# Window attention: scores and transposes in smaller array tiles, probabilities three quarters behind, work reordered

## The reference, cut to what matters

```python
x = roll(gn(x), (-3, -3))                       # cut in 7x7 windows: 16 * 64 of them
qkv = xw @ qkv_w.T + qkv_b                      # q, k, v: 12 heads of 16 channels
attn = einsum('bhnd,bhmd->bhnm', q * 16**-0.5, k) + bias[None] + mask
attn = softmax(attn, axis=-1)                   # 49 x 49 per head and window
out = einsum('bhnm,bhmd->bhnd', attn, v) @ proj_w.T + proj_b
x = x + roll(out, (3, 3))
```

## Time and profile before

| | us |
|---|---|
| median of 3 runs (4780.85 to 4781.38) | 4781.35 |
| profiled execution, its own time | 4778.66 |
| its span in the trace | 4776.7 |
| PE busy in the span | 4503.8 (94%) |
| DVE busy | 3946.8 (83%) |
| ACT busy | 2366.2 (50%) |
| POOL busy | 2379.3 (50%) |

### The profile page before, as it was taken

The page is one execution under the profiler, slowest core; times in us unless marked ns, Lnnn a source line. Parts: engine busy times, 40 slices in busy tenths (PEclk is TensorE's granted clock), DMA queues, the critical chain, the costliest instruction groups (busy, mean ns, idle before and its releaser), DMA issues. The chain is left out here.

```text
span 4776.7 us, 123308 instructions
## 1 busy us (share of the span) xinstructions
PE 4503.8 (94%) x42504; PEld 3833.8 (80%) x42504; DVE 3946.8 (83%) x7850; ACT 2366.2 (50%) x4594; POOL 2379.3 (50%) x2098
## 2 busy tenths in 40 slices
PE   0599999999999999999969999999999999999998
PEld 0488888888888888888857888888888888888887
DVE  6788888888888888888827888888888888888887
ACT  0244444444444444444415555555555656555565
POOL 1245554555555554555425555555555555555555
PEclk9999999999999999999969999999999999999999
DMA  8011111111111111111112222222222222222222
GB/s 341 21 38 39 39 41 38 38 39 39 41 37 39 39 41 37 39 40 41 34 40 67 69 68 69 69 67 71 67 70 69 68 68 69 70 68 70 67 70 59
DMA packets 397987, 285.95 MB, mean 60 GB/s; under 512 B 155355, under 2 KB 396235, under 8 KB 396747
## 3 DMA queue, kind: packets, MB, share of 16 engines
q1 hardware_dynamic: 395204, 283.19, 20.2%
q10 hardware_dynamic: 2736, 2.14, 0.1%
HBM read 120.34 MB, written 87.31 MB: 43 GB/s over the span
## 5 line engine op out<-in xcount | busy, mean ns | idle before, releaser
L882 POOL TENSOR_TENSOR E<-E,ri 128x588 f32<-128x588 f32 x512 | 646.3, 1262 | 1028.5 <-DVE ri L1107 1028.3
L602 PE MATMUL ps_o<-w,g_hi 128*128 128x384 f32 x2352 | 710.9, 365 | 5.9 <-DVE g_lo L542 4.1
L414 ACT ACTIVATE gF<-ps_g,b1f 128x512 f32<-128x512 f32 x588 | 404.7, 688 | 393.0 <-PE ps_g L633 390.7
L960 ACT ACTIVATE E<-L 128x588 f32<-128x588 f32 x512 | 356.1, 695 | 475.6 <-POOL L L888 242.5
L1097 DVE SCALAR_TENSOR_TENSOR L<-ps_s,bias 128x588 f32<-128x588 f32 x512 | 394.5, 770 | 178.0 <-PE ps_s L1241 161.9
L602 PE MATMUL ps_o<-w,g_lo 128*128 128x192 f32 x2352 | 534.8, 254 | 0.0
L1249 PE MATMUL ps_t<-ident,E 128*98 128x128 f32 x3072 | 441.3, 280 | 41.1 <-POOL E L882 41.1
L441 POOL TENSOR_TENSOR res<-xt,b2b 128x768 f32<-128x768 f32 x98 | 181.5, 1852 | 591.1 <-DVE x L490 591.1
L400 ACT ACTIVATE h_hi<-ps_h,hbias 128x512 fp32r<-128x512 f32 x196 | 123.1, 679 | 703.7 <-PE ps_h L617 703.7
L1249 PEld LDWEIGHTS ps_t<-ident,E 128*98 128x98 f32 x3072 | 313.4, 127 | 195.4 <-POOL E L882 108.3
L1241 PE MATMUL ps_s<-Kp,Q 64*64 64x196 f32 x6144 | 455.4, 342 | 2.7 <-DMA Kp<-K 2.7
(11 more groups left out here) (211 smaller groups left out, 12090.5 us busy)
## 6 DMA issues: line engine op xcount, KB each, us to landing
xs<-in_x SPq DMA_DIRECT2D x8, 4704.0 KB, 22.0
xt<-in_x SPq DMA_DIRECT2D x98, 384.0 KB, 3.4
x_cells<-x SPq DMA_DIRECT2D x784, 48.0 KB
xb<-x_cells SPq DMA_DIRECT2D x128, 294.0 KB
Vx<-V SPq DMA_DIRECT2D x512, 73.5 KB
out<-yo SPq DMA_DIRECT2D x128, 294.0 KB
Kp<-K SPq DMA_DIRECT2D x512, 49.0 KB, 1.9
Kp<-K SPq DMA_DIRECT2D x512, 24.5 KB, 1.8
```

Source lines behind the costliest of these rows:

```text
L414: act.activation(gF[f % 4][:, :], ps_g[:, f % 2, :], ACT.Gelu, bias=b1f[:, f:f + 1]).then_inc(s_gelu, 1)
L602: last = pe.matmul(dst, g[:, f, P * k:P * (k + 1)], w, start=(f == 0 and i == 0), stop=(f == FT - 1 and i == 1))
L882: pool.tensor_tensor(e, e, ri[p][:, :].unsqueeze(2).to_broadcast([P, HEADS, T]), ALU.mult)\
L960: act.activation(E[pp][:, :, :], L[pp][:, :, :], ACT.Exp).then_inc(s_ex, 1)
```

## The change

The scores are made in 32-row products of two heads (98 columns) instead of 64-row products of four (196): twelve products a quarter, in a first group of eight (head pairs at places 0, 3, 1, 4) and a second of four (places 2, 5), with the transposes between them. `PAIR_AT` says which head pair stands at which place. Two row groups that run together write to different banks of `ps_s`. The keys are spread over two heads' rows instead of four, so half as many DMAs with twice the rows each. The transposes take 64 rows (one window) each, window w to bank w of `ps_t`: twelve of 64 columns. The lag is three quarters. `mix` half 0 goes from p0 to p2, the second `turn` ahead of the values product of p0, the second `project` behind the values product of p1, the third and `values` half 0 behind that of p2. VectorE makes sums and reciprocals after the subtraction, the lower parts and the queries instead of before; GpSimd takes the maxima off before it multiplies; ScalarE copies PT before the exponentials. Banks and their waits follow. Weights, bias and the bias table are permuted on the way in. The core of the diff:

```diff
+PAIR_AT = (0, 4, 2, 1, 5, 3)
...
-            HB = HEADS // 3
-            QB = 256
+            HB = 2
+            SB = HEADS // 2 * T
...
-            OUT0, TURN, QK, VAL, OUT1 = 0, 1, 3, 6, 8
+            LAG = 3
+            TURN, KEYS, OUT0, QRY, VAL, OUT1 = 0, 2, 4, 5, 6, 8
...
+            def s_pair(j):
+                return ps_s[:, 2 * j // JP, T2 * (j % (JP // 2)):T2 * (j % (JP // 2) + 1)]
+            def pair_rows(g):
+                return slice(2 * HD * (g % PA), 2 * HD * (g % PA + 1)), g // PA
...
# GpSimd
+                        if is_unit(u):
+                            less_max(u, p)
                         if is_unit(pu):
                             norm(pu, pp)
-                        if is_unit(u):
-                            less_max(u, p)
...
# ScalarE, order in a quarter
+ evacuated 1 (p2); PT copy; E; upper 0, upper 1 (p0); evacuated 0 (p1); V copy (p3); oT; evacuated 2 (p2)
- E; evacuated 1 (p2); PT copy; evacuated 0 (p1); evacuated 2 (p2); V copy (p3); upper 0 (p0); oT; upper 1 (p0)
# VectorE, order in a quarter
+ L; mx; first heads less mx; lower 0, 1 (p0); queries_b (p1); sm, ri; finish 0, V copy (p2); finish 1 (p3)
- L; mx; sm, ri; first heads less mx; finish 0 (p0); lower 0, 1 (p0); queries_b (p1); V copy (p2); finish 1 (p3)
...
# TensorE
+                def scores(c, p, places):
+                    for j in places:
+                        rows, chunk = pair_rows(PAIR_AT[j])
+                        for w in range(2):
+                            last = pe.matmul(s_pair(j)[SLOT * w:SLOT * (w + 1)], Q[c][rows, chunk, 2 * p + w, :],
+                                             Kp[c][rows, chunk, :, 2 * p + w, :], start=True, stop=True)
+                    return last
...
                         if is_unit(lu):
                             pe.wait_ge(s_nm, k + 1)
                             upto(pe, s_ptc, k)
+                        if is_unit(u):
+                            if p == 0:
+                                pe.wait_ge(s_qkm, 3 * u + 3)
+                                pe.wait_ge(s_qb, u + 1)
+                                pe.wait_ge(s_kp[c], 16 * K_SPREADS * (i + 1))
+                            upto(pe, s_lg, UP * u + p)
+                            scores(c, p, (0, 3, 1, 4)).then_inc(s_scx, 1)
+                        if is_unit(lu):
                             for j in range(JP):
-                                last = pe.transpose(ps_t[0:T2, j // JB, P * (j % JB):P * (j % JB + 1)],
-                                                    E[lp][:, 2 * j:2 * j + 2, :].rearrange("p h m -> p (h m)"),
-                                                    ident[:, :])
+                                for w in range(2):
+                                    rows = slice(SLOT * w, SLOT * (w + 1))
+                                    last = pe.transpose(ps_t[0:T2, w, SLOT * j:SLOT * (j + 1)],
+                                                        E[lp][rows, 2 * j:2 * j + 2, :].rearrange("p h m -> p (h m)"),
+                                                        ident[rows, rows])
                             last.then_inc(s_pt, 1)
+                        if nxt and p == 0:
+                            pe.wait_ge(s_xb[1 - c], 16 * LOADS * (i + c + 1))
+                            for h in range(2):
+                                upto(pe, s_vc[h], v)
+                        if is_unit(u):
+                            pe.wait_ge(s_scx, UP * u + p + 1)
+                            scores(c, p, (2, 5)).then_inc(s_sc, 1)
-                        if is_unit(u - 1) and p == 0:
+                        if is_unit(u - 1) and p == 2:
                             mix(i, c, 0)
# then: turn 0, 1 (p0); project 0 (p1); values 1 (p3); values product; project 1 (p1); project 2, values 0 (p2); mix 1 (p3)
```

More of the change, by code:

```diff
@@ L935, in evacuated @@
                     v, d, m = 2 * i + c + 1, 1 - c, CHUNK_OF[step]
-                    full = ps_w(QK + step)[:, 0:UW].rearrange("p (w t) -> p w t", t=T)
+                    full = ps_qk(step)[:, 0:UW].rearrange("p (w t) -> p w t", t=T)
                     act.wait_ge(s_qk, 3 * v + step + 1)
@@ L991, in slot @@
                             last.then_inc(s_o, 1)
-                        if nxt and p == 0:
-                            upper(i, c, 1)
+                        if nxt and p == 2:
+                            evacuated(i, c, 2)
                 units(act, slot)
@@ L1166, in _ @@
                 pe.wait_ge(s_pad, 2)
-                def turn(i, c, h):
[L1171 to L1178, removed]
+                def scores(c, p, places):
[5 more added lines that the diff above has]
+                    return last
+                def turn(i, c, h):
+                    d, rows = 1 - c, CB if h else P
                     for p in range(UP):
@@ L1188, in project @@
                         pe.wait_ge(s_xl, 2 * v + 2)
-                        upto(pe, s_yo, 2 * (v - 2) + 1)
+                        upto(pe, s_yo, 2 * (v - 2))
+                    if step == 2:
+                        pe.wait_ge(s_qkm, 3 * v + 1)
+                        pe.wait_ge(s_qb, v + 1)
                     terms = W_QKV.terms(x_hi, x_lo, slice(P * m, P * (m + 1)))
                     for k, (w, x) in enumerate(terms):
-                        last = pe.matmul(ps_w(QK + step)[:, 0:UW], w, x, start=(k == 0), stop=(k == len(terms) - 1))
+                        last = pe.matmul(ps_qk(step)[:, 0:UW], w, x, start=(k == 0), stop=(k == len(terms) - 1))
                     last.then_inc(s_qk, 1)
@@ L1196, in values @@
                     v = 2 * i + c + 1
-                    pe.wait_ge(s_qkm, 3 * v + half + 1)
                     if half == 0:
-                        pe.wait_ge(s_qb, v + 1)
+                        pe.wait_ge(s_qkm, 3 * v + 2)
+                    else:
+                        upto(pe, s_yo, 2 * (v - 2) + 1)
                     for a in range(2):
@@ L1211, in mix @@
                     pe.wait_ge(s_o, UP * v + 2 * half + 2)
-                    if not is_unit(v + 2):
-                        pe.wait_ge(s_vc[0], UNITS)
+                    if is_unit(v + 2):
+                        if half == 0:
+                            pe.wait_ge(s_xl, 2 * (v + 2) + 2)
+                        else:
+                            pe.wait_ge(s_qkm, 3 * (v + 2) + 3)
+                    else:
+                        pe.wait_ge(s_vc[1], UNITS)
+                        pe.wait_ge(s_qkm, 3 * UNITS)
                         pe.wait_ge(s_yo, 2 * v)
[L1216 to L1219, removed]
                     for a in range(2):
@@ L1232, in slot @@
                         lu, lc, lp = lagged(u, c, p)
[L1233 to L1243, removed]
+                        k = UP * u + p - LAG
@@ L1288, in slot @@
                             last.then_inc(s_pv, 1)
-                        if nxt and p == 0:
-                            turn(i, c, 1)
-                        if nxt and p == 3:
-                            pe.wait_ge(s_qkm, 3 * (u + 1) + 3)
-                            pe.wait_ge(s_qb, u + 2)
-                            pe.wait_ge(s_kp[1 - c], 16 * K_SPREADS * (i + c + 1))
+                        if nxt:
+                            if p == 1:
+                                project(i, c, 1)
+                            if p == 2:
+                                project(i, c, 2)
+                                values(i, c, 0)
                         if is_unit(u - 1) and p == 3:
@@ L1367 @@
     arrays["b1"] = by_column(inputs["L0_conv_b1"], rows=P)[:, :, 0]
-    def by_dimension(block):
-        return CB * block + np.array([HD * e + d for d in range(HD) for e in range(CB // HD)])
-    first, second = np.r_[by_dimension(0), by_dimension(2)], by_dimension(1)
+    by_dimension = np.array([2 * HD * g + HD * e + d for g in range(JP) for d in range(HD) for e in range(2)])
+    first, second = by_dimension[0:P], by_dimension[P:C]
     by_parity = np.array([HD * (2 * j + e) + d for e in range(2) for d in range(HD) for j in range(JP)])
@@ L1379 @@
     arrays["proj_b"] = plain("L1_conv_proj_b")
-    arrays["rpb"] = plain("L1_conv_rpb_table")
+    arrays["rpb"] = np.ascontiguousarray(plain("L1_conv_rpb_table")[:, [2 * g + e for g in PAIR_AT for e in range(2)]])
     arrays.update(shape_constants())
```

101 lines of the change are left out of this document (44 added, 57 removed).

## The result

The changed kernel takes 4791.9 us (median of 20 runs, 4787.5 to 4794.0), the kernel before 4781.5 (20 runs). The ratio is 1.0021, 95% interval 1.0015 to 1.0027: 0.2% slower, clear of the noise, where 4741 and faster was forecast.

What follows compares the result with a forecast made beforehand. TensorE, busy 2055 of 2100 us, was taken to bound the attention stage. Work of 16.77 plus a 0.54 stall, less a few hundredths, gave 17.28 a unit: 0.32 x 127 = 41 us gained, 4741 on the median's scale; range 4690 to 4825.

Steps and rivals of the forecast that it cites:

- The signs that the prediction named: Unit 17.3 us, no p2 probability wait, about 0.5 gap before first projection, transposes under 0.4 between starts, first scores 0.32.
- Small tiles: TensorE, each quarter: scores plus transposes become 0.50 + 0.54 + 0.33 = 1.37 us against 1.44; block behind gains 0.03 more.
- Rival A: TensorE weight loads of parts in other rows queue: transposes 0.72, +0.38 a quarter, +104 us, 4885; chance 0.16.
- the low end of 0.51: Transposes: shortest block considered, at 0.06 us a step, against the 0.54 taken.
- The order's work: TensorE blocks reordered over p0 to p3, split projections 1.04 each: work alone 16.77 us a unit against 16.9.
- nothing: Values product: visiting array parts in another order costs nothing, as the fullest part keeps 8 of 24 matmuls.
- the bound of 0.13 a quarter: Values product: two steps, 0.13 us, if a taken array part holds up the free ones behind it.
- The wait that comes: First projection of p1: TensorE, there after 4.18 us, stands 0.54 for VectorE's x_lo, ready at 4.72.
- Followed to the end of the unit no other wait is last.: Rest of the unit, all engines: besides the x_lo wait, no other wait would hold TensorE.
- a wait for heads: TensorE in p0 before the change: 0.08 us behind the transposes (0.70 for 0.62), read as waiting for heads from ScalarE.
- Rival D: Some other engine's order (GpSimd behind the residual, PV's order) takes 0.3 or more a unit: 4780 to 4820; chance 0.14.
- C: First projection of p1: the x_lo wait doesn't hold TensorE, so work decides; -112 us, 4669; chance 0.12.

Runs made afterwards that it cites:

- order and two: The kernel of "all three" with scores back to six 64-row products in one group and transposes to six of 128 rows; 4863.4 us, ratio 1.0163.
- residual first: The changed kernel with GpSimd in p0 adding the residual before it multiplies the exponentials, instead of after; 4775.0 us, ratio 0.9987.
- residual in p1: The changed kernel with p0 lower parts before subtraction, values product by array parts, and GpSimd's residual in p1 between subtraction and multiplication; 4689.6 us.
- all three: The changed kernel with residual before multiplication and lower parts before subtraction in p0, and values product in array-part order; 4820.5 us, ratio 1.0075.
- lag two: The kernel of "all three" with transposes and values product two quarters behind their scores instead of three; 6072.3 us, ratio 1.2695.

## Why the prediction was wrong

The forecast gain was 0.32 us a unit; the measured unit lost 0.14. The signs that the prediction named came (waits on the probabilities gone, the largest wait ahead of the first projection, transposes 0.33 from first to last start), all but the unit itself: 17.74 for 17.3. Step by step:

- **Small tiles.** The shapes run side by side as assumed. Rival A is dead: the block of transposes takes 0.47, less than the low end of 0.51, its steps some 0.055. The Trainium skill's rule for weight loads, columns over 1.2 per ns (TensorE: Matmul & The Clock Gate, LDWEIGHTS), would make 98 columns take 0.082; the trace disagrees again. I undervalued the tiles: 0.1 a quarter forecast, 0.15 by the blocks of "order and two". The 0.07 a quarter by which the transposes beat their 0.54 is the only term that came out better.
- **The order's work.** Values product: "nothing" was wrong, over 0.04 a quarter, 0.13 where it counts; the bound of 0.13 a quarter stood in the text. Each half of the split projections is 1.09 to 1.10 instead of 1.04, 0.11 a unit: a first step in a new shape of 392 columns is 0.1 longer than the following ones, not 0.05. The third projection has the same first step, 0.05 more.
- **The wait that comes.** Right in place and cause, and undersized: 0.74 for 0.54. From p0's start to the first projection 4.82 instead of 4.72, although the transposes give 0.07 back. Logits start 0.07 behind the scores instead of 0.04, and from first to second lower part it is 0.66 instead of 0.54: the second waits for ScalarE's upper part in none of the rows; it starts 0.04 behind the end of the first, where an overlap of 0.08 was forecast.
- **"Followed to the end of the unit no other wait is last."** This failed, and it is the step that turned the sign. I followed GpSimd's residual into what GpSimd does next and not into what VectorE does beside it. Its subtraction was costed at the earlier trace rows's 0.40 and took 1.87; the delay reaches `finish` half 0, moved behind the sums by the same change, and through it the values of p3, 0.15 a unit. The run "residual first" undoes this alone and lands at 4775, the faster side of before.
- **Sum.** Chain 0.10, values product 0.13, split projections 0.11, `finish` 0.15, rests 0.12 (the third projection, the values of p3, and the hundredths taken off for sharper starts), less 0.15 for the transposes of p2 and p3: 0.46 over the forecast 17.28, which is the 17.74 measured. No single one is large; all stand against a gain of 0.32. Without the 0.15 of `finish` the unit would be 17.59, a hair under the old 17.60: that term turned the sign, and the others ate the gain. The first units of the stage give some 5 us back (15.2 and 13.8 us, where they took 17.3 and 15.5), so that 127 x 0.14 became 10; from the last p0 to the end it is 47 us in both kernels.
- **A wait that likely was none.** The prediction reads 0.08 behind the transposes of p0 as a wait for heads. In "order and two" the same 0.70 stands behind the transposes ahead of turn too, which needs no heads, and where the output projection follows them, it is 0.08 shorter (1.40 for 1.47). This changed nothing in the sum.
- **Rival D** comes nearest ("some other engine's order, GpSimd behind the residual, PV's order"). It named both places with a chance of 0.14 and a price by guess. C was wrong: the stall holds TensorE. Those two places make 0.28 of the 0.46; the time lies in D's range only with the other terms added, so that much is luck.

With "residual in p1" the same way of adding closes: 16.65 of work (16.77 was forecast) and 0.29 of stall make 16.94.

## What to carry to other kernels

Before a reordering is costed, list which operations of VectorE and GpSimd will now run at the same time, not only which wait for which: here a subtraction with two SBUF operands on VectorE and the sum on GpSimd went one after the other. Where several small stalls lie on one chain, removing one shows little, since the next takes it over (0.50 less in one stall was 0.13 less in the unit); judge each by its own row and then test them together. And a combination can meet in a place where neither part did: 4775, 4774 and 4788 alone, 4820 together, 4690 with one instruction moved a quarter on.

## What the runs showed of the hardware

VectorE's subtraction with two SBUF operands does not proceed during GpSimd's sum: it ended 0.32 us behind it, both when started 0.27 and when started 0.50 us after its start (means of 119 and 118 units in the changed kernel and in "all three"). The Trainium skill (SBUF — State Buffer, Terms) calls the port pair of the two an exclusive lock held for the whole instruction, in which "the loser fully blocks"; the trace agrees, with 1.87 us for an operation of 0.40. Reductions (0.77 us), and the logits that read one operand from PSUM (0.73 to 0.77), show no such lengthening beside GpSimd.

The order in which the parts of the array are given work counts: the same twelve products take 0.66 us in the order 0 0 2 1 1 3 and 0.615 in the order 0 1 2 3 0 1. By which mechanism no run shows. Transposes of 64-row halves come in steps of about 0.055 us with both halves at work (0.54 for the block, less 0.22 for the last one and 0.05 for the longer first step, over five). Where the shape changes, the next block begins 0.07 us before the modelled end of the last matmul, in every kind of block here. TensorE's granted clock was 1.00 in this stretch before and after the change and 0.80 in "lag two", where the engine was busy 73%; behind a wait of 4.4 us its scores took 0.93 instead of 0.57.
